# Attention's out projections as three products of high and low parts, and a new order for the end of attention

## The chip, the cores and the metric

The kernel runs on one core of one Trainium2 chip. The metric is the time of one execution on the device, in microseconds. The engines are PE (TensorE), ACT (ScalarE), DVE (VectorE), POOL (GpSimd) and SP (SyncE, which only issues DMAs here). Each runs its own instructions in program order, and they meet at semaphores.

## The reference

```python
x = x + 0.5 * ffn(layernorm(x))     # 2048 tokens of 512; top 2 of 8 experts, 256 wide, all in float32
x = x + attn(layernorm(x))          # 16 query heads, 4 key and value heads of 32, rope, causal
x = x + 0.5 * ffn(layernorm(x))
# attn: q, k, v = x @ wq, x @ wk, x @ wv; rope on q, k
#       softmax(q k^T / sqrt(32), causal) v, heads side by side, then @ wo (512 x 512)
# ffn:  logits = x @ router_w.T; softmax over the top 2; silu(x w1) * (x w2) @ w3 of each
```

The out projection, `out @ wo`, is what the change is about. Its result, added to x, decides which experts each token gets in the second ffn, so it is wanted in nearly full float32.

## The kernel before

The program is five stages: the first router, 39 expert tiles, the projections of Q, K and V, attention with the second router, and 39 expert tiles again. A product of full precision is written in one of two ways. The plain one is a float32 matmul. The other splits both factors into a high part in fp32r (ScalarE's copy that rounds) and a low part (the factor minus the high part) and sums three fp32r matmuls, high x high, high x low and low x high; the experts (L839, L862) are written so.

Attention works through 16 groups G (query block b = G // 4 of 512 tokens, key head G % 4 with its 4 query heads). A group has 4b + 4 tiles, one for each 128 keys. A tile is four steps `score` (PE L1635, then ACT's exp L1754 into P4, of which there are 2 up to group 7 and 4 from group 8), and one `weigh` a tile later (PE L1647, P times V). Where the sums of exps are formed differs: PE (L1665), POOL's `link` adds into CH (L1827, k = 1, 2, 4, 5, 7 and from block 3 on 8, 10), DMA's `onto` adds into CD (L1843), and in group 15 DVE's `pair` (L1891). POOL also masks the four diagonal tiles of each group (L1813). While groups run, PE also computes `top` products for the row maxima of later groups (L997; DVE L1010, L1012); the last one is at 962 us.

At a group's end `out` copies the weighted values to OT and the sums to SM (ACT L1762, L1765), `tsum` turns the sums (PE L1673, DVE reciprocal L1904), `even` spreads them (PE L1682) and DVE multiplies OT (L1914; in group 15 in four pieces, L1918). After a block's fourth group follows its finish: four `proj` of 128 tokens (PE L1702, 4 chunks of the 512 inputs), DVE's add of x (L1877, L1879), statistics, normalization, four `turn` (PE L388, ACT L399), `logits` and `best`.

The order is one hand-written list, `attend_plan`, that each engine's loop walks through, doing its own share of each step. `finish_plan` gives a block's finish, of which one entry is taken per tile, at its second score; the finish of block 0 begins 34 steps after its last group, those of blocks 1 and 2 nine steps after, in the fourth tile of groups 8 and 12. The end of attention (block 3) is written out at the end of `attend_plan`: after the last `weigh` come `out` 15, four splits of weights for the second experts (`split1`: ACT L567 high, then POOL L573 low), `tsum`, `even` and, for each c of 4, `proj`, `norm1` (DVE: statistics, variance; ACT's root L340; DVE's Newton steps and the shift L1952) and `scale1` (ACT L1774); `keep` copies the sum from PSUM to XO (ACT L1781) and frees its bank. `pe_turn` 15 is preceded by 11 filler matmuls (L378).

PSUM's eight banks: `Ring` hands out banks to steps in the order of the plan, from a list that `set_banks` changes; whoever is given a bank waits until its former user has freed it (`pe_take`). Bank 3 holds the weighted values, 4 the sums; scores use three banks, and five from the last `top` on.

OT is two buffers, one for even and one for odd blocks. WO, the weights, is loaded by SP before the first score.

## Time and profile before

| | us |
|---|---|
| three runs | 1288.40, 1294.34, 1295.16 |
| median | 1294.34 |
| profiled execution, its own time | 1291.39 |
| its span, first to last instruction | 1290.1 |
| PE busy in the span | 1198.4 (93%) |
| DVE busy | 891.7 (69%) |
| ACT busy | 665.4 (52%) |
| POOL busy | 599.7 (46%) |
| mean granted TensorE clock | 0.987 of 2.4 GHz |
| attention: first score to the router's logits | 417.5 to 1048.9 |
| PE's out projections, 64 matmuls as 128 records | 57.4 busy, 0.59 each |

The profile has each instruction with its start and duration, and for idle time the work whose end released it. A float32 matmul stands as two records; matmuls overlap, so a step's cost is the distance between starts, not the sum of the durations. Busy shares over the whole span say little about a change in one stage, so the rows below are read by stage.

### The profile page before, as it was taken

What the parts mean: (1) busy time and instruction counts of PE and PEld (TensorE: products, weight loads), DVE (VectorE), ACT (ScalarE), POOL (GpSimd) and SP (SyncE); (2) the same over time, 40 slices, a digit from 0 to 9 for tenths busy, and PEclk for the clock granted to TensorE, in tenths of its full rate; (3) what the DMA queues carried; (4) which work ended last, traced back from release to release, by engine and by line L of the source; (5) the groups of instructions that cost most, each with busy time, mean ns of one, the idle gap of its engine ahead of it and who ended that gap; (6) DMA issues with size and microseconds to landing.
All of it is one profiled execution on the core that took longest, in us unless ns stands there. A gap on an engine that the chain in (4) does not pass through costs nothing.

```text
span 1290.1 us, 22099 instructions
## 1 busy us (share of the span) xinstructions
PE 1198.4 (93%) x7406; PEld 778.3 (60%) x7413; DVE 891.7 (69%) x2100; ACT 665.4 (52%) x1321; POOL 599.7 (46%) x496
## 2 busy tenths in 40 slices
PE   4899999999998999999999999989999978999996
PEld 3578888758776555444545455545444446777774
DVE  7767777679996666476577677677763666666664
ACT  2545555436555554354456565456567853444442
POOL 4845444323210111001436457454764273888886
PEclk9899999999999999999999999999999999999998
DMA  9933333565630032023445844655843263666665
GB/s 331 364 97 107 106 108 108 169 178 107 101 57 5 32 68 35 1 69 67 98 99 147 173 108 99 197 120 146 162 98 67 69 236 85 102 106 101 101 103 78
DMA packets 68557, 148.52 MB, mean 115 GB/s; under 512 B 8832, under 2 KB 29312, under 8 KB 64448
## 3 DMA queue, kind: packets, MB, share of 16 engines
q0 software_dynamic: 35184, 93.34, 34.3%
q1 hardware_dynamic: 33264, 53.77, 12.2%
q8 instruction: 64, 1.05, 0.3%
q14 instruction: 45, 0.37, 0.1%
HBM read 81.28 MB, written 33.55 MB: 89 GB/s over the span
## 4 chain that ended last, share of the span: by engine, by line
PE 61%; DVE 15%; DMA 10%; issue 6%; POOL 4%; ACT 4%; SPq 0%; DVEq 0%; POOLq 0%; ACTq 0%
PE bank L839 10%; PE bank L1635 10%; PE bank L1647 9%; PE bank L997 8%; PE bank L862 6%; PE bank L1702 4%; PE bank L1665 4%; DMA XG<-xn,TK 4%; POOL out L789 3%; DMA out<-Y,DI 3%; DVE PM L1010 3%; DVE bank L1012 2%; PE bank L821 2%; PE bank L1398 2%; DMA CD<-P 1%
## 5 line engine op out<-in xcount | busy, mean ns | idle before, releaser
L1754 ACT ACTIVATE P<-bank 128x512 f32<-128x512 f32 (+3 forms) x640 | 303.6, 535 | 259.3 <-PE bank L1635 252.7
L1010 DVE TENSOR_REDUCE PM<-bank 128x1 f32<-128x512 f32 x384 | 252.8, 686 | 82.6 <-PE bank L997 81.9
L1635 PE MATMUL bank<-Qs,Ks 98*128 98x512 f32 (+3 forms) x640 | 241.0, 407 | 5.1 <-ACT P L1754 2.8
L997 PE MATMUL bank<-Ks,Qs 96*128 96x512 f32 (+3 forms) x640 | 234.4, 387 | 10.8 <-DVE PM L1012 5.3
L1635 PEld LDWEIGHTS bank<-Qs,Ks 98*128 98x128 f32 x640 | 116.8, 190 | 130.8 <-issue 59.5
L1813 POOL TENSOR_SCALAR_AFFINE_SELECT P<-P 128x512 f32<-128x512 f32 x64 | 42.7, 677 | 284.6 <-ACT P L1754 235.2
L1012 DVE CUSTOM_DVE_ANT_0 bank<-bank,KB 128x128 f32<-128x128 f32 (+3 forms) x256 | 124.7, 499 | 56.4 <-PE bank L997 55.8
L997 PEld LDWEIGHTS bank<-Ks,Qs 96*128 96x128 f32 x640 | 121.5, 191 | 57.5 <-DVE PM L1010 17.5
L1647 PE MATMUL bank<-P,V 128*32 128x512 f32 (+3 forms) x1280 | 150.9, 543 | 3.7 <-POOL P L1813 3.7
L1827 POOL TENSOR_TENSOR CH<-CH,P 128x512 f32<-128x512 f32 x108 | 139.2, 1435 | 14.1 <-ACT P L1754 13.3
L789 POOL DMA_INDIRECT out<-Y,DI x78 | 126.1, 1617 | 38.4 <-issue 29.4
L951 DVE TENSOR_TENSOR DL<-W,DH 128x512 fp32r<-128x512 f32 x152 | 98.4, 689 | 40.9 <-issue 20.5
L766 POOL DMA_INDIRECT XG<-xn,TK x78 | 93.5, 1198 | 32.7 <-issue 18.9
L912 ACT CAST DH<-W 128x512 fp32r x152 | 86.7, 618 | 20.3 <-issue 20.3
L839 PE MATMUL bank<-WH,XH 128*128 x312 | 92.3, 417 | 0.9 <-issue 0.6
L839 PE MATMUL bank<-WL,XH 128*128 x312 | 85.7, 396 | 1.4 <-DVE XL L933 1.4
L778 POOL DMA_INDIRECT y<-Y,DI x39 | 40.5, 1039 | 97.3 <-DVE Y L961 97.3
L839 PE MATMUL bank<-WH,XL 128*128 x312 | 85.4, 395 | 0.0
L933 DVE TENSOR_TENSOR XL<-bank,XH 128x512 fp32r<-128x512 f32 x78 | 53.9, 691 | 32.3 <-ACT XH L892 32.1
L898 ACT ACTIVATE G<-bank 128x256 f32<-128x256 f32 x78 | 29.9, 384 | 85.5 <-PE bank L839 85.5
L892 ACT CAST XH<-bank 128x512 fp32r<-128x512 f32 x78 | 45.8, 587 | 43.9 <-PE bank L821 41.2
L839 PEld LDWEIGHTS bank<-WL,XH 128*128 128x128 f32 x312 | 58.6, 188 | 15.9 <-issue 1.8
(195 smaller groups left out, 1978.1 us busy)
## 6 DMA issues: line engine op xcount, KB each, us to landing
CD<-P POOLq DMA_DIRECT2D x17, 1024.0 KB, 7.3
xn<-XN SPq DMA_DIRECT2D x8, 1024.0 KB, 6.5
WR<-L_ffn_w POOLq DMA_DIRECT2D x16, 512.0 KB, 15.6
XO<-y POOLq DMA_DIRECT2D x8, 1024.0 KB, 9.6
WR<-L_ffn_w SPq DMA_DIRECT2D x16, 512.0 KB, 8.4
CD<-P SPq DMA_DIRECT2D x7, 1024.0 KB, 5.2
CD<-CH POOLq DMA_DIRECT2D x7, 1024.0 KB, 6.9
XA<-y POOLq DMA_DIRECT2D x24, 256.0 KB, 4.2
```

Of the source, the lines that this page charges most:

```text
L766: pool.indirect_dma_start(out=x.XG[:, j % NG, :], out_offset=None, in_=g.xnd[f][:, :], in_offset=bass.IndirectOffsetOnAxis(ap=r.TK[:, j:j ...
L789: pool.indirect_dma_start(out=g.out.rearrange("t (h d) -> (t h) d", h=2), out_offset=bass.IndirectOffsetOnAxis(ap=r.DI2[:, h, j:j + 1], ax ...
L839: ins = pe.matmul(bk(g, 2 + j % 2), part[:, k * P:k * P + P], w[:, bass.ds(ev[j] * 2048 + k * 512, 512)], start=(n == 0 and k == 0), stop= ...
L912: act.copy(x.DH[:, k, :], W.W3[:, bass.ds(e * 1024 + k * 512, 512)]).then_inc(s("dh"), 1)
L951: ins = dve.tensor_tensor(x.DL[:, k, :], W.W3[:, bass.ds(e * 1024 + k * 512, 512)], DHf[:, k, :], ALU.subtract)
L997: pe.matmul(bk(g, bank)[:, 0:n], g.Qs[b][0:96, G % 4 * 4 + h, c * P:c * P + P], g.Ks[0:96, G % 4, k * BQ:k * BQ + n], start=True, stop=Tru ...
L1010: dve.tensor_reduce(dst, bk(g, bank)[:, 0:n], AX.X, ALU.max).then_inc(s(f"free{bank}"), 1)
L1012: dve.tensor_tensor_reduce(out=bk(g, bank)[:, 0:n], in0=bk(g, bank)[:, 0:n], in1=g.KB[:, CB_MASK + BQ - n:CB_MASK + BQ], scale=1.0, scalar ...
L1635: pe.matmul(bk(g, bank)[:, o:BQ], g.Ks[0:98, G % 4, k * P:k * P + P], g.Qs[G // 4][0:98, G % 4 * 4 + j, o:BQ], start=True, stop=True).then ...
L1647: ins = pe.matmul(bk(g, 3)[32 * h:32 * h + 32, o:BQ], g.V[:, k, q * HD:q * HD + HD], a.P4[buffer_of(n)][:, h, o:BQ], start=(k == 0), stop= ...
L1754: act.activation(a.P4[buffer_of(n)][:, j, o:BQ], bk(g, score_bank(g, i))[:, o:BQ], ACT.Exp, scale=scale).then_inc(s("exp"), 1)
L1827: ins = pool.tensor_tensor(to[:, h, :], two[:, h, :], one[:, h, :], ALU.add)
```

## The change

The out projections of blocks 1 to 3 are computed by three fp32r products each. During block 0's finish ACT copies the four chunks of WO to WOH and POOL subtracts to WOL; WOH lies over OT0, WOL over WO. From then on all blocks use OT1, with its low part OL in the same place and its high part OH in place of the turned xT1. The step `part` makes a quarter of OH (ACT) and of OL (POOL). Blocks 1 and 2 have a quarter per 128 tokens, and their projections begin two tiles later than the parts; block 3 has a quarter per group, after the tiles (14, 4), (14, 9) and (15, 6), and group 15's own quarter is made by DVE, in `late`, from the bank where `even` wrote.

At the end, the first three chunks of block 3's projections are steps of their own (`lead`): those of c = 0 in the three tiles before the last one's `weigh`, the others around `tsum`, `even` and the later projections. `proj` 3 is left with the chunk of group 15. `norm1` is cut in two, with `var1` (statistics, variance, root) ahead; `late`, `var1`, `norm1`, `split1`, `keep` and `turn` stand in a new order, and the ring's lists of banks are others. SP's loads of WO and XO count on one semaphore, `rows`. POOL's `part` in the diff is cut; it picks the same quarter as ACT's. The walks over the plan call the new functions, and ACT's root stands at `var1`.

```diff
@@ memory(nc, ctx, g)
     a.XO = low("XO", [P, 4, D])
-    a.OTs = [ot0, low("OT1", [P, 4, BQ])]
+    a.WOH = nc.alloc_sbuf_tensor_at("WOH", [P, 4, D], F32R, offset=A_T + 16 * KB1)
+    a.WOL = nc.alloc_sbuf_tensor_at("WOL", [P, 4, D], F32R, offset=A_T + 24 * KB1)
+    a.OL = nc.alloc_sbuf_tensor_at("OL", [P, 4, BQ], F32R, offset=low.at)
+    ot1 = low("OT1", [P, 4, BQ])
+    a.OTs = [ot0, ot1, ot1, ot1]
+    a.OH = nc.alloc_sbuf_tensor_at("OH", [P, 4, 4, P], F32R, offset=low.at + 8 * KB1)
@@ finish_plan(b)
-    todo = [[("proj", b, c)] for c in range(4)]
-    todo += [[("stats", b, c)] for c in range(4)]
+    if b:
+        todo = [[("part", b, 0)], [("part", b, 1)], [("part", b, 2), ("proj", b, 0)], [("part", b, 3), ("proj", b, 1)],
+                [("proj", b, 2)], [("proj", b, 3)]]
+        todo += [[("stats", b, c)] for c in range(4)]
+    else:
+        todo = [[("proj", b, c)] for c in range(4)]
+        todo += [[("stats", b, c), ("wo", c)] for c in range(4)]
@@ attend_plan(g)
+        if (G, k) in ((14, 4), (14, 9), (15, 6)):
+            plan.append(("part", 3, {4: 0, 9: 1, 6: 2}[k]))
+        if len(TILES) - 4 <= n < len(TILES) - 1:
+            put(4 * n + 7, ("lead", 0, n + 4 - len(TILES)))
-    plan += [("weigh", len(TILES) - 1), ("out", 15), ("up1", 4), ("split1", 0), ("split1", 1), ("split1", 2), ("split1", 3), ("tsum", 15), ("even", 15)]
-    for c in range(4):
-        plan += [("proj", 3, c), ("norm1", c), ("scale1", c)] + ([("turn", 12 + c - 2), ("keep", c - 2)] if c >= 2 else [])
-    plan += [("turn", 14), ("turn", 15), ("keep", 2), ("keep", 3), ("split1", 4), ("split1", 5), ("split1", 6), ("split1", 7)]
+    plan += [("weigh", len(TILES) - 1), ("out", 15), ("up1", 4), ("split1", 0), ("split1", 1), ("split1", 2)]
+    plan += [("lead", 1, 0), ("tsum", 15), ("lead", 1, 1), ("even", 15), ("late", 0), ("late", 1), ("lead", 1, 2)]
+    plan += [("proj", 3, 0), ("var1", 0), ("late", 2), ("proj", 3, 1), ("norm1", 0), ("scale1", 0), ("late", 3), ("var1", 1), ("split1", 3)]
+    plan += [("lead", 2, k) for k in range(3)] + [("proj", 3, 2), ("norm1", 1), ("scale1", 1), ("var1", 2), ("turn", 12), ("keep", 0)]
+    plan += [("lead", 3, k) for k in range(3)] + [("proj", 3, 3), ("norm1", 2), ("scale1", 2), ("var1", 3), ("turn", 13)]
+    plan += [("norm1", 3), ("scale1", 3), ("keep", 1), ("turn", 14), ("turn", 15), ("keep", 2), ("keep", 3)]
+    plan += [("split1", 4), ("split1", 5), ("split1", 6), ("split1", 7)]
-        if step == ("proj", 3, 0):
-            ring.set_banks([5, 6, 7, 0, 2, 1], 5)
+        if step == ("turn", 12):
+            ring.set_banks([6, 0, 7, 5], 3)
         elif step == ("out", 15):
-            ring.set_banks([5, 6, 7])
+            ring.set_banks([5, 6, 0, 1, 2], 4)
+        elif step[0] == "lead" and step[2] == 0:
+            ring.take(("proj", 3, step[1]))
@@ pe_attend(g)
+    def times_wo(bank, c, k):
+
+        pe.matmul(bk(g, bank), a.OH[:, c, k, :], a.WOH[:, k, :], start=(k == 0), stop=False)
+        pe.matmul(bk(g, bank), a.OH[:, c, k, :], a.WOL[:, k, :], start=False, stop=False)
+        return pe.matmul(bk(g, bank), a.OL[:, k, c * P:c * P + P], a.WOH[:, k, :], start=False, stop=(k == 3))
+
+    def lead(c, k):
+
+        bank, _ = g.ring.where[("proj", 3, c)]
+        if k == 0:
+            pe_take(g, ("proj", 3, c))
+            if c == 0:
+                b0, u0 = g.ring.where[("even", 14)]
+                pe.wait_ge(s(f"free{b0}"), u0 + 1)
+            else:
+                pe.wait_ge(s("exp"), 4 * len(TILES))
+            pe.wait_ge(s("ol"), 15)
+        times_wo(bank, c, k)
+
+    def last_proj(key):
+
+        _, b, c = key
+        bank, _ = g.ring.where[key]
+        if c < 3:
+            pe.wait_ge(s("ol"), c + 16)
+        else:
+            b0, u0 = g.ring.where[("even", 15)]
+            pe.wait_ge(s(f"free{b0}"), u0 + 1)
+        times_wo(bank, c, 3).then_inc(s(f"full{bank}"), 1)
+
     def proj(key):
...
+        if b:
+            pe.wait_ge(s("ol"), 4 * b + c + 1)
+            for k in range(4):
+                ins = times_wo(bank, c, k)
+            ins.then_inc(s(f"full{bank}"), 1)
+            return
         for k in range(4):
-            ins = pe.matmul(bk(g, bank), a.OTs[b % 2][:, k, c * P:c * P + P], a.WO[:, k, :], start=(k == 0), stop=(k == 3))
+            ins = pe.matmul(bk(g, bank), a.OTs[b][:, k, c * P:c * P + P], a.WO[:, k, :], start=(k == 0), stop=(k == 3))
         ins.then_inc(s(f"full{bank}"), 1)
@@ act_attend(g)
         if b >= 2 and G % 4 == 0:
-            bank, use = g.ring.where[("proj", b - 2, 3)]
+            bank, use = g.ring.where[("proj", b - 1, 3)]
             act.wait_ge(s(f"full{bank}"), use + 1)
-        act.copy(a.OTs[b % 2][:, G % 4, :], bk(g, 3)).then_inc(s("oT"), 1)
+        act.copy(a.OTs[b][:, G % 4, :], bk(g, 3)).then_inc(s("oT"), 1)
+    def part(b, i):
+
+
+        b0, u0 = g.ring.where[("even", 4 * b + 3 if b < 3 else 12 + i)]
+        act.wait_ge(s(f"free{b0}"), u0 + 1)
+        if i == 0:
+            b1, u1 = g.ring.where[("best", 1, b - 1)]
+            act.wait_ge(s(f"full{b1}"), u1 + 1)
+        if b < 3:
+            act.copy(a.OH[:, i, :, :], a.OTs[b][:, :, i * P:i * P + P]).then_inc(s("oh"), 1)
+        else:
+            act.copy(a.OH[:, :, i, :], a.OTs[b][:, i, :].rearrange("p (c n) -> p c n", c=4)).then_inc(s("oh"), 1)
+
+    def weights(k):
+        if k == 0:
+            bank, use = g.ring.where[("proj", 0, 3)]
+            act.wait_ge(s(f"full{bank}"), use + 1)
+        act.copy(a.WOH[:, k, :], a.WO[:, k, :]).then_inc(s("oh"), 1)
@@ pool_attend(g)
+    def part(b, i):
+
+        pool.wait_ge(s("oh"), 4 * b + i + 1)
...
+        pool.tensor_tensor(to, one, high.bitcast(F32), ALU.subtract).then_inc(s("ol"), 1)
+
+    def weights(k):
+        pool.wait_ge(s("oh"), k + 1)
+        pool.tensor_tensor(a.WOL[:, k, :], a.WO[:, k, :], a.WOH[:, k, :].bitcast(F32), ALU.subtract).then_inc(s("ol"), 1)
@@ dve_attend(g)
-        for c in range(4):
-            v = slice(c * P, c * P + P)
-            ins = dve.tensor_tensor(o[:, v], o[:, v], bk(g, bank)[:, v], ALU.mult)
-            ins.then_inc(s("norm") if c < 3 else s(f"free{bank}"), 1)
+
+    def late(c):
+
+        bank, use = g.ring.where[("even", 15)]
+        o, v = bk(g, bank)[:, c * P:c * P + P], slice(c * P, c * P + P)
+        dve.tensor_tensor(o, a.OTs[3][:, 3, v], o, ALU.mult).then_inc(g.dv.sem, 1)
+        dve.wait_ge(g.dv.sem, g.dv.up())
+        dve.tensor_copy(a.OH[:, c, 3, :], o).then_inc(g.dv.sem, 1)
+        dve.wait_ge(g.dv.sem, g.dv.up())
+        ins = dve.tensor_tensor(a.OL[:, 3, v], o, a.OH[:, c, 3, :].bitcast(F32), ALU.subtract)
+        ins.then_inc(s("ol") if c < 3 else s(f"free{bank}"), 1)
```

## Rows read from the trace of the kernel before

**Rows 1.** Busy time of each engine in two stretches: busy us (instructions), clock, DMA share, GB/s.
```profile
820.00:860.00 40.00, 38.25 (x170) 19.64 (x169) 27.67 (x63) 17.87 (x34) 27.48 (x23) 1.00 0.48 114
965.00:1015.00 50.00, 47.19 (x334) 19.76 (x334) 25.35 (x42) 41.01 (x86) 16.00 (x16) 1.00 0.26 53
```
**Rows 2.** POOL's timeline, groups 12 and 14: start, us, what; idle before and its releaser.
```profile
842.83 0.85 POOL L1843 DMA_DIRECT2D CD<-P  x1 [5.13 <-ACT P L1754]
...
951.08 10.07 POOL L1827 TENSOR_TENSOR CH<-CH,P 128x512 f32<-128x512 f32 x8 [0.53 <-ACT P L1754]
...
961.73 10.26 POOL L1827 TENSOR_TENSOR CH<-CH,P 128x512 f32<-128x512 f32 x8
...
972.52 5.23 POOL L1827 TENSOR_TENSOR CH<-CH,P 128x512 f32<-128x512 f32 x4
977.47 0.85 POOL L1813 TENSOR_SCALAR_AFFINE_SELECT P<-P 128x512 f32<-128x512 f32 x1
```
**Rows 3.** PE's timeline, the diagonal tiles of group 14.
```profile
978.47 1.06 PE L1647 MATMUL bank<-P,V 128*32 128x512 f32 x8 [1.20 <-POOL P L1813]
...
986.22 1.07 PE L1656 MATMUL bank<-CD,ones 128*32 128x512 f32 x8 [0.36 <-DMA CD<-CH]
```
**Rows 4.** PE's timeline from the last tiles to the router's logits.
```profile
1016.63 1.06 PE L1647 MATMUL bank<-P,V 128*32 128x512 f32 x8 [0.64 <-POOL P L1813]
...
1022.57 0.43 PE L1647 MATMUL bank<-P,V 128*32 128x128 f32 x8 [0.33 <-POOL P L1813]
...
1025.91 1.08 PE L1682 MATMUL bank<-K,R 128*32 128x128 f32 x32 [0.42 <-DVE R L1904]
1027.49 10.54 PE L1702 MATMUL bank<-WO,OT 128*128 128x512 f32 x24 [0.50 <-DVE OT L1918]
...
1043.93 2.32 PE L378 MATMUL bank<-KB 128*128 128x512 bf16 x10
1047.12 0.63 PE L388 MATMUL bank<-K,XN 128*128 128x128 f32 x4 [0.87 <-ACT XO L1781]
1048.91 1.54 PE L413 MATMUL bank<-xT,RT 128*32 128x128 f32 x32 [1.16 <-ACT XO L1781]
```
**Rows 5.** PE's timeline, four fp32r products of an expert.
```profile
1078.24 1.10 PE L839 MATMUL bank<-WL,XH 128*128 x4
```
**Rows 6.** ACT's timeline, the last scaling and what follows.
```profile
1045.24 0.78 ACT L1774 ACTIVATE XN<-bank,sm 128x512 f32<-128x512 f32 x1 [1.23 <-DVE sm L1952]
...
1046.38 0.60 ACT L1781 COPY XO<-bank 128x512 f32<-128x512 f32 x1
...
1048.27 1.08 ACT L1781 COPY XO<-bank 128x512 f32<-128x512 f32 x2
```
**Rows 7.** DVE's timeline behind the last `even`.
```profile
1027.06 0.88 DVE L1918 TENSOR_TENSOR OT<-OT,bank 128x128 f32<-128x128 f32 x4 [1.20 <-PE bank L1682]
1031.20 0.70 DVE L1879 TENSOR_TENSOR bank<-bank,XO 128x512 f32<-128x512 f32 x1 [3.26 <-PE bank L1702]
...
1034.63 0.70 DVE L1879 TENSOR_TENSOR bank<-bank,XO 128x512 f32<-128x512 f32 x1
...
1036.74 0.16 DVE L327 RECIPROCAL sm<-sm 128x1 f32<-128x1 f32 x1 [0.27 <-ACT sm L340]
```
**Rows 8.** PE's timeline, a hole in the stage of the projections of Q, K, V.
```profile
412.48 3.96 PE L1415 MATMUL bank<-K,NA 128*96 128x128 f32 x20 [2.67 <-DVE NA L1271]
```
**Rows 9.** Stretches as in the first group; the 1.00 or 0.50 is the clock.
```profile
413.00:414.00 1.00, 1.00 (x7) 0.93 (x5) 0.00 (x0) 0.78 (x3) 0.00 (x0) 0.50 0.00 0
416.00:417.00 1.00, 0.44 (x5) 0.18 (x2) 0.00 (x0) 0.96 (x2) 0.00 (x0) 1.00 0.00 0
672.00:673.00 1.00, 1.00 (x3) 0.77 (x3) 0.41 (x3) 0.82 (x2) 0.47 (x1) 0.50 0.00 0
677.00:678.00 1.00, 1.00 (x13) 0.59 (x6) 0.00 (x0) 0.25 (x1) 0.00 (x0) 0.50 0.00 0
1046.00:1048.00 2.00, 0.88 (x6) 0.42 (x4) 0.00 (x0) 1.68 (x5) 0.00 (x0) 1.00 0.55 214
```

More of the change, by code:

```diff
@@ L1594, in attend_plan @@
             ring.set_banks(ids, len(ids) - 1)
-        if step[0] in ("top", "proj", "tsum", "even", "found"):
+        if step[0] in ("top", "tsum", "even", "found") or step[0] == "proj" and step[1] < 3:
             ring.take(step)
+        elif step[0] == "lead" and step[2] == 0:
+            ring.take(("proj", 3, step[1]))
         elif step[0] in ("turn", "logits", "best"):
@@ L1689, in proj @@
         if b == 0 and c == 0:
-            pe.wait_ge(s("wo"), 16)
+            pe.wait_ge(s("rows"), 32)
         b0, u0 = g.ring.where[("even", 4 * b + 3)]
@@ L1720, in pe_attend @@
             even(step)
+        elif kind == "proj" and step[1] == 3:
+            last_proj(step)
         elif kind == "proj":
             proj(step)
+        elif kind == "lead":
+            lead(step[1], step[2])
         elif kind == "turn":
@@ L1792, in act_attend @@
             out(step[1])
+        elif kind == "part":
+            part(step[1], step[2])
+        elif kind == "wo":
+            weights(step[1])
         elif kind == "foundcopy":
@@ L1843, in onto @@
         pool.dma_start(a.CD[:], one[:], accum_op=ALU.add).then_inc(s("onto"), 16)
-    for step in g.plan:
-        if step[0] == "score" and step[2] == 3:
+    def part(b, i):
+        pool.wait_ge(s("oh"), 4 * b + i + 1)
+        if b < 3:
+            to, one = (t[:, :, i * P:i * P + P] for t in (a.OL, a.OTs[b]))
+            high = a.OH[:, i, :, :]
+        else:
+            to, one = (t[:, i, :].rearrange("p (c n) -> p c n", c=4) for t in (a.OL, a.OTs[b]))
+            high = a.OH[:, :, i, :]
+        pool.tensor_tensor(to, one, high.bitcast(F32), ALU.subtract).then_inc(s("ol"), 1)
+    def weights(k):
+        pool.wait_ge(s("oh"), k + 1)
+        pool.tensor_tensor(a.WOL[:, k, :], a.WO[:, k, :], a.WOH[:, k, :].bitcast(F32), ALU.subtract).then_inc(s("ol"), 1)
+    for step in g.plan:
+        if step[0] == "part":
+            part(step[1], step[2])
+        elif step[0] == "wo":
+            weights(step[1])
+        elif step[0] == "score" and step[2] == 3:
             n = step[1]
@@ L1858, in pool_attend @@
             else:
-                pool.wait_ge(s("xo"), 16 * b + 16)
+                pool.wait_ge(s("rows"), 16 * b + 32)
             pool.dma_start(a.XO[:], g.yd[T * h + BQ * b:T * h + BQ * b + BQ, :].rearrange("(i p) d -> p i d", p=P),
@@ L1944, in dve_attend @@
             dve_scale(g, g.R1, step[1], a.XO, step[2])
-        elif kind == "norm1":
-            c, sm = step[1], g.R1.sm
+        elif kind == "late":
+            late(step[1])
+        elif kind == "var1":
+            c = step[1]
             dve.wait_ge(s("last"), c + 1)
@@ L1950, in dve_attend @@
             dve_variance(g, g.R1, c, c + 1, 3 + c)
+        elif kind == "norm1":
+            c, sm = step[1], g.R1.sm
             dve_solve(g, g.R1, c, c + 1, 3 + c)
@@ L1962, in sp_attend @@
     all_projected(g, sp.wait_ge)
-    sp.dma_start(a.WO[:], d["L0_attn_wo"].rearrange("(k p) n -> p k n", p=P)).then_inc(s("wo"), 16)
+    sp.dma_start(a.WO[:], d["L0_attn_wo"].rearrange("(k p) n -> p k n", p=P)).then_inc(s("rows"), 16)
     def rows(t, b):
@@ L1985, in sp_attend @@
                 sp.wait_ge(s("stored"), 16 * b)
-            sp.dma_start(a.XO[:], rows(d["L0_attn_x"].rearrange("b t d -> (b t) d"), b)).then_inc(s("xo"), 16)
+            sp.dma_start(a.XO[:], rows(d["L0_attn_x"].rearrange("b t d -> (b t) d"), b)).then_inc(s("rows"), 16)
         elif kind == "store":
```

12 lines of the change are left out of this document (3 added, 9 removed).

## The prediction, made before the changed kernel was run

> **What bounds the kernel now.** I read the busy time by stage first, then PE's timeline at the out projections, then POOL's, and last every engine from the final score tile to the router's logits. While tops still run, PE is busy 38.25 of 40 us and no other engine comes near; from 965 to 1015 us, once they are gone, ACT has 41 of 50 us and PE 47 [rows 1]. So whatever PE saves before 965 us shortens the span, one for one, unless a later wait takes it back. Two places are not PE's. In group 14 POOL works from 951 to 978 us without a break and PE and ACT wait for it [rows 2, 3]. From the last score on, the work is a chain through ACT, PE and DVE, and its steps decide.
>
> **Projections of blocks 1 and 2 (a gain).** The plain form of one projection leaves eight records of PE; 24 records, three projections, take 10.54 us, each 0.59 long, so they start (10.54 - 0.59) / 23 = 0.433 us apart and a projection is 3.46 us of PE [rows 4]. The new form is twelve fp32r products of 128 x 512. The experts already run that form: four take 1.10 us, the last 0.395 of it, so one costs (1.10 - 0.395) / 3 = 0.235 us [rows 5], and twelve 2.82. Saved: 0.64 us each, 5.1 us for the eight of blocks 1 and 2. Bounds: 0 (if DVE's tops or ACT take over at once) and 5.6 us. I take 5.1, as PE is the busy engine there.
>
> **What that form adds.** ACT gets 15 copies of 128 x 512 (4 weights, 8 for blocks 1 and 2, 3 for block 3), POOL 15 subtractions. A copy is 0.6 us by ACT's COPY to XO [rows 6]; a POOL add of that size is 5.23 / 4 = 1.3 us [rows 2]. In block 0's finish POOL only masks, and ACT has more than half of the time free; in groups 8 and 12 the parts come at tiles 3 to 6, where POOL still waits (5.13 us idle just before 842.83 [rows 2]), so four parts, 5.2 us, fill holes. Behind them on POOL stand links 4, 5 and 7, whose buffers are wanted four tiles later, and the first projection moves two tiles back to wait for its parts. Cost 0, up to 1.5 us without that cover. The shared OT1 makes group 8's and 12's copy wait for projection 3 of the block before; that is over three tiles earlier. The joined semaphore of SP's loads, and the finish that is two tiles longer, cost nothing: stores and XO loads have tens of us.
>
> **Parts of block 3 in group 14 (a loss).** Two of the three parts are planned after tiles 4 and 9 of group 14. There POOL has 10.07, 10.26 and 5.23 us of adds with two DMA issues between them, end to end, and then the mask that PE waits 1.20 us for [rows 2, 3]. Queued behind the parts are links 5, 7, 8 and 10, the DMA adds, the masks. Two parts at 1.25 us are 2.5 us; the later wait for the merged sum (0.36 us on PE) is there before and is absorbed [rows 3], so +2.1. Bounds 0 and 3.0. The third part is in group 15, where POOL only masks.
>
> **First products in the last tiles (a loss ahead, a gain behind).** `lead` 0 is 9 of projection 0's 12 products, three in each of the last tiles: 3 x 0.70 = 2.1 us. Two holes of PE take 0.64 and 0.33 of it [rows 4]; +1.1. Projection 1's three leads lie in the waits around `tsum` and `even`; the middle one is 0.70 long against a hole of 0.4 and so delays `even` by 0.2. Together +1.3, bounds +0.6 and +2.1.
>
> **From `even` 15 to the last shift (a gain).** Before, DVE begins at 1027.06, the first sum waits for the whole projection 0 (3.26 us idle) and starts at 1031.20, and the last shift is out at 1045.24, 18.2 us after 1027.06 [rows 6, 7]. One chunk is 3.43 us of DVE (1031.20 to 1034.63), 0.27 us of the next one is the wait for the root [rows 7]. Behind, DVE is the bound: four `late` of three operations at 0.28 and two self waits, 0.93 each, 3.7; four chunks 13.7; three root waits, now under other work, -0.8: 16.6 us. PE, three products after each `late`, stays ahead of it. So -1.6.
>
> **From the last shift to the logits (a loss).** Here the banks matter. Going through the ring by hand: projection 1 sits in bank 5, projection 3 in bank 0, and turns 12 to 15 get 6, 7, 5, 6, the logits 0. So turn 14 needs `keep` 1, which ACT does only after `scale_last` 3; the 11 filler matmuls of turn 15 are behind turn 14 on PE; and the logits need `keep` 3, not 2. Before, turn 14 and the filler (2.32 us for ten) ran under the last chunk, turn 15 began 1.88 us after the shift and the logits 3.67 us after it [rows 4, 6]. Behind: scale 0.7, keep 0.6 and hand-over, turn 14 at +1.4; turn 0.63 and filler 2.4, turn 15 at +4.45; from there 1.8 as before and one more copy of 0.5: logits at +6.8. That is +3.1; bounds +1.5 and +3.6.
>
> **TensorE's clock.** On that schedule PE has nothing between turn 13 (about 12.5 us after `even`) and turn 14 (18.0), 5.5 us. After a hole of 2.67 us before 412.48 the granted clock was 0.50, that is 1.2 GHz, at 413 us, and 1.00 again at 416 [rows 8, 9]. Turn 14 and filler, 3.0 us, would so run at half for up to 3.3 us: +1.3 (0 to 1.7). The Trainium skill (TensorE: Matmul & The Clock Gate, Part 1: The HAM clock gate) says that the half-rate state is the default and activity lifts it, in two levels only; by that rule this change, which leaves PE less to do at the end, pays for it in the work that follows. The trace agrees: 0.50 in the rows named, and nothing between the levels but slices that hold both.
>
> **Sum.** -5.1 + 2.1 + 1.3 - 1.6 + 3.1 + 1.3 = +1.1 us. The profiled execution took 1291.39 us; it lies 2.95 us under the median of the three runs, 1294.34, and these spread over 6.8 us. The profile's differences carry over to the median: 1295.4 us.
>
> **Rivals.**
> (A) POOL and the end cost nothing. If POOL's parts in group 14 pass under ACT's own waits, and the turns come in a better order than I read, the body's gain stays: -5.1 + 0 + 1.3 - 1.6 + 1.5 = -3.9, 1290.4 us. With the body at 5.6, the leads at 0.6 and nothing at the turns it would be -6.6, 1287.7 us, the only way to be clearly faster. For it: PE is the bound nearly everywhere. Against: POOL's unbroken row in group 14.
> (B) Slower: the clock falls in both holes of the end. PE also has 2 us without work before turn 12, which waits for the first `scale_last`, and `lead` 3 stands behind turn 12. In its place the loss is this: a half clock that lasts 6 us, as at 672 and 677 us [rows 9], doubles `lead` 3 with its last products (2.8 us more, 1.9 of it past DVE's own time), and at the other hole turn 14, the filler, turn 15 and the logits (2.4 + 0.5 + 0.5 + 1.5 = 4.9). 6.8 in place of 1.3: +6.6, 1300.9 us. It decides once the clock falls before `lead` 3. Before, the end kept 1.00 through holes of 0.9 us [rows 4, 9], which speaks against it; the 2 us hole speaks for it.
> (C) The change does not bring its gain in the body: DVE, 27.67 of 40 us busy [rows 1], or ACT behind the new copies holds PE, and 5.1 becomes 0: +6.2, 1300.5 us. Little speaks for it, as PE hardly waits there now.
>
> **How the numbers follow.** Forecast 0.50, (A) 0.28, (B) 0.14, (C) 0.08. About 0.5%, 6.5 us, is what a measurement of this kernel can tell from no change: 1287.9 to 1300.8. All of the forecast's case, most of (A) and half of (B) and (C) lie within. Range 1287.5 to 1302: down to (A) at its best, up to (B), a little over. Faster 0.14, same 0.70, slower 0.16.
>
> **What would show it.** Right: PE's out projections in groups 8 and 12 as twelve records at 0.235 us; POOL's row in group 14 ends 2.5 us later and PE's wait for the mask grows from 1.20 to some 3.7; the first sum of block 3 starts 2 us after `even` 15 where it was 4.1; the last shift is 16.6 us after it; PE idle over 5 us before turn 14, waiting for ACT's copy to XO, then a granted clock of 0.5. Wrong: a PE wait for POOL's low part at a projection in group 8 or 12; PE at DVE's mercy in the body; turn 14 directly after turn 13.

## The result, and the profile after

The changed kernel takes 1298.23 us (median of ten runs, 1296.07 to 1300.47), the kernel before 1292.70 us in the same session (ten runs, 1288.40 to 1296.12). The ratio is 1.004, with an interval of 1.0026 to 1.0053. The forecast was 1295.4, between 1287.5 and 1302; the time lies in the range and within 0.5%. Its direction, a little slower, is right. The change itself was forecast at 1.1 us and measured at 5.5. That the time still lies within 0.3% of the forecast is partly luck: the forecast started from the median of three runs, 1294.34, and ten runs of the kernel before have 1292.70. The last experiment says how little a ratio of this size can carry.

The page of the changed kernel, its busy times and one row of its slices:

```profile
span 1297.5 us, 22237 instructions
PE 1198.1 (92%) x7454; PEld 794.7 (61%) x7461; DVE 895.9 (69%) x2108; ACT 672.0 (52%) x1336; POOL 621.7 (48%) x511
...
PEclk8899999999998999999999999999998979999999
```

Before, the span was 1290.1 us and PE busy for 1198.4. So PE works as long as before although the projections got shorter: it does some of its work at half the clock. ACT has 15 operations more, POOL 15.

The first two rows below answer to [rows 1]: the same stretch of group 12 and of groups 14 and 15, counted from the sums (`tsum`) before them. The columns are those of [rows 1]. In the first PE is as busy as before, and POOL has 3.7 us more (31.15 for 27.48), where the low parts are. In the second PE has lost 2.6 us of work in 50 (44.60 for 47.19), and its clock is 0.93. The last two lie in the end of attention.

```profile
819.00:859.00 40.00, 38.30 (x194) 24.10 (x193) 28.31 (x62) 20.28 (x39) 31.15 (x26) 1.00 0.51 124
960.50:1010.50 50.00, 44.60 (x309) 18.27 (x305) 21.27 (x34) 37.32 (x80) 20.13 (x19) 0.93 0.28 58
...
1044.00:1046.00 2.00, 1.54 (x6) 1.17 (x8) 0.00 (x0) 0.68 (x2) 1.28 (x1) 0.50 0.76 295
1046.00:1048.00 2.00, 2.00 (x6) 0.71 (x5) 0.00 (x0) 0.00 (x0) 0.00 (x0) 0.50 0.60 229
```

One profile of each isn't enough for differences of a few us, so both kernels were profiled again, before three times and the changed one once. Landmarks on PE's timeline cut the span into stages; a stage `gN` runs from the transposed sum (`tsum`) of group N - 1 to that of group N. The experts' first is PE's first turn of gated values in the second expert stage. Worked out from those timelines, in us, as means of four profiles and of two:

```
stage                        before   after   difference   forecast
start to first score          417.3   417.5      +0.2          0
first score to tsum 0          17.0    17.8      +0.7          0
g1 to g6 (same work)          150.9   150.9       0            0
g7                             34.9    34.5      -0.4          0
g8                             58.1    54.7      -3.4        -2.6
g9                             47.1    49.6      +2.5          0
g10, g11 (same work)           82.5    82.4       0            0
g12                            72.8    67.8      -5.0        -2.6
g13                            57.9    59.3      +1.3          0
g14                            47.7    51.6      +3.9        +2.1
g15                            36.4    37.5      +1.1        +1.1
tsum 15 to logits              24.1    26.6      +2.6        +3.0
logits to experts' first       32.4    31.9      -0.6          0
second experts and end        210.7   213.3      +2.7          0
span                         1289.9  1295.4      +5.6        +1.1
```

So the body (g8, g9, g12, g13) gave 4.6 us, forecast 5.1; group 14 took 3.9 in place of 2.1; group 15 and the end took 3.6 in place of 4.1. What the forecast had no term for at all is the last stage, +2.7.

PE's timeline of the changed kernel, a projection in group 8 (columns as in [rows 3]). These are twelve records where there were eight, the first three and the last shown:

```profile
635.91 0.40 PE L1709 MATMUL bank<-WOH,OH 128*128 128x512 f32 x1
636.15 0.40 PE L1710 MATMUL bank<-WOL,OH 128*128 128x512 f32 x1
636.38 0.39 PE L1711 MATMUL bank<-WOH,OL 128*128 128x512 f32 x1
...
638.43 0.39 PE L1711 MATMUL bank<-WOH,OL 128*128 128x512 f32 x1
```

From 635.91 to the next score at 638.65 it is 2.74 us; the forecast had 2.82.

PE's timeline in the groups 9 and 14 of the changed kernel. The first two rows are the transposed sum that ends group 8 and the transposed row maxima in group 9; before waited 0.42 and 0.82 us there. The third answers to the first of [rows 3], 1.20 there; the 0.36 that followed it is gone. The last row is a stretch of PE alone behind it (its busy time, the clock, DMA share, GB/s).

```profile
677.31 0.89 PE L1694 MATMUL bank<-K,SM 128*128 128x128 f32 x4 [2.64 <-DVE PM L1017]
...
697.22 0.60 PE L1066 MATMUL bank<-K,M 128*8 128x128 f32 x4 [2.70 <-DVE M L1057]
...
976.40 1.93 PE L1668 MATMUL bank<-P,V 128*32 128x512 f32 x8 [4.53 <-POOL P L1892]
...
976.00:981.00 5.00, 4.60 (x20) 0.50 0.77 159
```

In front of the first two waits stands DVE's normalization of block 1: at the end of group 8 DVE waits for ACT's root, and in group 9 a scaling takes 1.68 us, where most take 0.54, ahead of the last reductions.

```profile
675.55 0.18 DVE L319 RECIPROCAL sm<-sm 128x4 f32<-128x4 f32 x1 [1.10 <-ACT sm L347]
...
693.13 1.68 DVE L361 TENSOR_SCALAR XN<-XO,mv,sm 128x512 f32<-128x512 f32 x1
```

The eight products at 976.40 take 1.93 us where eight of the same form took 1.06 in [rows 3]: half the clock. POOL's timeline of the same place, with the two low parts (L1933) in a row that was already full [rows 2]:

```profile
951.62 1.29 POOL L1933 TENSOR_TENSOR OL<-OT,OH 128x512 fp32r<-128x512 f32 x1
952.86 5.00 POOL L1906 TENSOR_TENSOR CH<-CH,P 128x512 f32<-128x512 f32 x4
...
958.39 10.35 POOL L1906 TENSOR_TENSOR CH<-CH,P 128x512 f32<-128x512 f32 x8
...
969.23 1.56 POOL L1933 TENSOR_TENSOR OL<-OT,OH 128x512 fp32r<-128x512 f32 x1
970.47 5.20 POOL L1906 TENSOR_TENSOR CH<-CH,P 128x512 f32<-128x512 f32 x4
975.37 0.89 POOL L1892 TENSOR_SCALAR_AFFINE_SELECT P<-P 128x512 f32<-128x512 f32 x1
```

The end of attention, which answers to [rows 4]. PE of the changed kernel from turn 12 to the logits:

```profile
1035.03 0.66 PE L395 MATMUL bank<-K,XN 128*128 128x128 f32 x4 [1.51 <-ACT XN L1849]
...
1040.05 0.63 PE L395 MATMUL bank<-K,XN 128*128 128x128 f32 x4 [1.62 <-ACT XO L1856]
1044.24 1.09 PE L395 MATMUL bank<-K,XN 128*128 128x128 f32 x4 [3.56 <-ACT XO L1856]
1045.55 4.35 PE L385 MATMUL bank<-KB 128*128 128x512 bf16 x10 [0.22 <-issue]
...
1051.98 1.54 PE L420 MATMUL bank<-xT,RT 128*32 128x128 f32 x32 [1.65 <-ACT XO L1856]
```

Turn 14 (1044.24) waits for `keep` 1, which ACT does behind the last scaling. Then ten filler matmuls take 4.35 us; in [rows 4] they took 2.32. DVE and ACT (which answer to [rows 6, 7]), the same kernel: the first product with the normalizer (`late` 0), the first sum, the sums of chunks 2 and 3, the last shift, the last scaling, and `keep` 1.

```profile
1027.82 0.30 DVE L2018 TENSOR_TENSOR bank<-OT,bank 128x128 f32<-128x128 f32 x1 [1.41 <-PE bank L1703]
...
1029.81 0.70 DVE L1977 TENSOR_TENSOR bank<-bank,XO 128x512 f32<-128x512 f32 x1 [0.20 <-PE bank L1711]
...
1035.94 0.69 DVE L1977 TENSOR_TENSOR bank<-bank,XO 128x512 f32<-128x512 f32 x1
1036.54 0.15 DVE L334 RECIPROCAL sm<-sm 128x1 f32<-128x1 f32 x1
...
1038.62 0.69 DVE L1977 TENSOR_TENSOR bank<-bank,XO 128x512 f32<-128x512 f32 x1
...
1042.59 0.21 DVE L2060 TENSOR_SCALAR sm<-mv,sm 128x1 f32<-128x1 f32 x1
...
1042.84 0.78 ACT L1849 ACTIVATE XN<-bank,sm 128x512 f32<-128x512 f32 x1 [0.76 <-DVE sm L2060]
1043.52 0.58 ACT L1856 COPY XO<-bank 128x512 f32<-128x512 f32 x1
```

The first sum starts 1.99 us after `late` 0, and the last shift is out at 1042.80, 15.0 us after it. A chunk is 1038.62 - 1035.94 = 2.68 us of DVE, for 3.43 before. Of that 3.43, DVE waited 0.43 for the root, in this row of the kernel before:

```profile
1033.46 0.16 DVE L327 RECIPROCAL sm<-sm 128x1 f32<-128x1 f32 x1 [0.43 <-ACT sm L340]
```

### The profile page after: what moved, and what is told of

Its sections match the earlier page's. It is cut to its first block, busy times and chain, and to the rows that moved or that the text cites. A ratio compares the mean times of both kernels' runs of the same rounds, so it can differ in the third digit from the quotient of the medians.

```text
span 1297.5 us, 22237 instructions
## 1 busy us (share of the span) xinstructions
PE 1198.1 (92%) x7454; PEld 794.7 (61%) x7461; DVE 895.9 (69%) x2108; ACT 672.0 (52%) x1336; POOL 621.7 (48%) x511
## 3 DMA queue, kind: packets, MB, share of 16 engines
q8 instruction: 64, 1.05, 0.3%
## 4 chain that ended last, share of the span: by engine, by line
PE 63%; DVE 16%; DMA 7%; issue 6%; POOL 5%; ACT 3%; SPq 0%; POOLq 0%; DVEq 0%; ACTq 0%
PE bank L846 10%; PE bank L1656 10%; PE bank L1668 9%; PE bank L1004 8%; PE bank L869 6%; PE bank L1686 4%; DMA out<-Y,DI 4%; DMA XG<-xn,TK 3%; DVE bank L1019 2%; DVE PM L1017 2%; POOL out L796 2%; PE bank L828 2%; POOL CH L1906 2%; PE bank L1405 2%; PE bank L1703 1%
## 5 line engine op out<-in xcount | busy, mean ns | idle before, releaser
L796 POOL DMA_INDIRECT out<-Y,DI x78 | 128.3, 1644 | 40.8 <-issue 30.5
L911 ACT CAST GH<-bank 128x256 fp32r<-128x256 f32 x76 | 28.3, 373 | 78.1 <-PE bank L856 71.9
```

Of the source, the lines that this page charges most:

```text
L796: pool.indirect_dma_start(out=g.out.rearrange("t (h d) -> (t h) d", h=2), out_offset=bass.IndirectOffsetOnAxis(ap=r.DI2[:, h, j:j + 1], ax ...
```

## The experiments

**Both kernels again, unchanged.** These give the stages above their spread.

> The kernel before, once more, for a second profile of it: the changed kernel's profile is 5.2 us longer in the second expert stage and 2.0 us in group 0, where the two run the same code. Theory (the stages vary from execution to execution by clock and gathers): the second expert stage, from the first to the last turn of gated values, is not 196.3 us again but 197 to 200, and group 0 ends 17 to 19 us after the first score. Rival (something in the changed kernel makes them longer): 196.3 +- 0.5 and 16.8 +- 0.3 us again.

> The kernel before, a third profile. The second expert stage, the same code in all kernels, took 196.3 and 197.2 us in two profiles of the kernel before and 197.6 to 201.5 in eight of the changed kernel and its variants. Theory (its gathers land at varying times, and the eight are chance): one of the three profiles of this call's kernels before falls above 198.5 or the changed kernel's below 198. Rival (the changed kernel really makes it longer): 196 to 197.5 here, 199 to 201 in the changed kernel.

> The kernel before, a fourth profile: as for the third, the second expert stage above 198.5 us by the one theory, 196 to 197.5 by the other. Groups 8 and 9 together 105 to 107 us, group 14 47.6 us and from group 15's sums to the logits 24.1 us again by both.

> The changed kernel, a second profile: group 14 51.5 us with a hole of 4.5 us before its first masked tile, and a half clock there and before the logits again (26.6 us from group 15's sums to the logits); the second expert stage below 198 us if its length is chance, 199 to 201 if the changed kernel makes it longer.

Measured: 1289.06, 1291.14 and 1292.86 us for before, 1294.64 us for the changed kernel; spans 1287.8, 1289.9, 1291.6 and 1293.4. Most stages agree to 0.1 us between profiles of one kernel; of those that don't, first score to `tsum` 0, g7, g8 and g12 differ by where the granted clock happened to be at half; the second experts differ by up to 3 us among the profiles of before. The changed kernel's first profile has 18.8 us between the first score and `tsum` 0, its second 16.8, with the same instructions. Group 14 repeats: 51.5 and 51.7, with 4.53 and 4.54 us of wait for the mask. So do g9 (49.6, 49.5), g13 (59.3, 59.3) and the end (26.6, 26.7). Those are of the change; the first +0.7 is not. Of the theories on the second experts' stage, neither holds cleanly: a fourth profile of before has 198.8 us from the first to the last turn of gated values, above the 198.5 that speaks for chance, and the changed kernel's second has 200.7, which speaks for the change.

**The low parts of block 3 out of group 14, into group 15.**

```
-        if (G, k) in ((14, 4), (14, 9), (15, 6)):
+        if (G, k) in ((15, 1), (15, 4), (15, 7)):
```

> The changed kernel with the three parts of block 3 all planned in group 15 (after tiles 1, 4 and 7), where GpSimd has nothing else to do but mask. Theory (GpSimd's two extra subtractions in group 14 push the mask that TensorE waits for, and the longer hole also lowers the granted clock): the wait before the weigh of group 14's first masked tile falls from 4.5 us to about 1.2, the half clock at 974 to 981 us is gone, and the kernel is about 3.9 us faster than the changed kernel, 1294.3 us, still 1 to 2 us above the kernel before. Rival (the loss in group 14 comes from TensorE being ahead by the projections' gain and would appear wherever the parts are): the time stays at 1298 us and the same wait is there. Second rival (in group 15 the subtractions meet VectorE's pair sums and ScalarE, 41 of 50 us busy): the mask of group 15 comes later by 1 to 2 us and takes back half of the gain.

Measured: 1295.01 us (12 runs), before 1292.17; ratio 1.0021 (1.0006 to 1.0036). Group 14 went from 51.6 to 49.9 us and the wait for the mask to 2.43, but group 15 from 37.5 to 40.1, some of it under a half clock (995 to 999 us). With the same edit in the third kernel below it is 48.5 and 38.8. This profile is of the slowest of the twelve executions (1302.15 us). So part of what POOL gave back in group 14, in this profile all of it, went in group 15, as the second rival said, and its rows show where. The median is near the theory's 1294.3, but its wait of 1.2 us is not there (2.43), and the half clock in group 14 is shorter, not gone (978 to 982 us). DVE in group 15 adds pairs of tiles, both inputs from SBUF; these are its rows here (duration in ns, least, median and most), and the same operation before:

```profile
L1989 DVE TENSOR_TENSOR CD<-CD,P x40: 635/684/1770, 994.9 to 1024.7; 128x512 f32<-128x512 f32 x40
L1989 DVE TENSOR_TENSOR CD<-P,P x4: 683/688/1756, 991.3 to 993.1; 128x512 f32<-128x512 f32 x4
```
```profile
L1891 DVE TENSOR_TENSOR CD<-CD,P x40: 643/686/1120, 991.7 to 1017.6; 128x512 f32<-128x512 f32 x40
```

An add of 0.69 us takes up to 1.77 when POOL subtracts beside it, and POOL's subtraction goes from 1.29 to as much as 1.79 (at 1010.36). One such add (between 991.29 and 994.78) delays the reciprocal of group 14's sums, and PE then waits for it:

```profile
995.17 1.48 PE L1703 MATMUL bank<-K,R 128*32 128x128 f32 x32 [1.80 <-DVE R L2002]
```

That wait was 0.87 us in the changed kernel. The Trainium skill (SBUF — State Buffer, section 🔬 SBUF: two separate sides) says that DVE and GpSimd share a port pair by an exclusive lock, held for a whole instruction, and that a DVE operation with two SBUF inputs meets it against a GpSimd operation that reads SBUF. With that the trace agrees: 1.77 us is 0.69 and most of one subtraction of 1.29.

**`keep` 1 ahead of the last scaling.**

```
-    plan += [("norm1", 3), ("scale1", 3), ("keep", 1), ("turn", 14), ...
+    plan += [("keep", 1), ("norm1", 3), ("scale1", 3), ("turn", 14), ...
```

> The changed kernel with one step moved: ScalarE's copy keep 1 stands right after turn 13, ahead of the last scaling. Theory (turn 14 waits for bank 5, which keep 1 frees after the last scaling; TensorE stands idle before it, and its clock falls under turn 14, the fillers and turn 15): turn 14 starts 1.5 us earlier, turn 15 and the logits 1.5 us earlier with the clock unchanged, up to 4 us earlier if the clock stays at 1.00; 1294 to 1297 us. Rival (the chain is set by VectorE's statistics and what comes behind them, the bank doesn't matter): logits at the same distance, 9.1 us, from the last shift, 1298 us.

Measured: 1294.79 us (12 runs), ratio 1.0020 (1.0000 to 1.0040). From `tsum` 15 to the logits it is 24.1 us, as before the change, in place of 26.6. PE's timeline, turns 14 and 15 and the logits:

```profile
1041.11 0.63 PE L395 MATMUL bank<-K,XN 128*128 128x128 f32 x4 [2.05 <-ACT XO L1856]
1041.57 4.22 PE L385 MATMUL bank<-KB 128*128 128x512 bf16 x11
1045.63 0.60 PE L395 MATMUL bank<-K,XN 128*128 128x128 f32 x4
1047.89 1.54 PE L420 MATMUL bank<-xT,RT 128*32 128x128 f32 x32 [1.65 <-ACT XO L1856]
```

Turn 14 starts at 1041.11, just as the last shift is done (1041.19), where that of the changed kernel starts 1.44 us behind it. Yet the eleven fillers still take 4.22 us. PE alone over two stretches (its busy time, the clock, DMA share, GB/s):

```profile
1040.00:1042.00 2.00, 0.89 (x6) 0.92 0.03 8
1042.00:1044.00 2.00, 2.00 (x6) 0.50 0.55 212
```

The clock is at half, and turn 15 waits behind them.

**Both together.**

> The changed kernel with both: the three parts of block 3 in group 15 and keep 1 right after turn 13. Theory: the two losses are apart from each other and their removal adds up, 5 to 7 us under the changed kernel, 1291 to 1293 us, level with the kernel before or 1 us under it. Rival (the loss lies elsewhere, in the second expert stage, which was 5.2 us longer in the changed kernel's profile): 1297 us or more.

Measured: 1296.62 us (12 runs), ratio 1.0032 (1.0015 to 1.0048). Group 14 is 48.5 us and group 15 38.8, the end 25.1; together 112.4, where the changed kernel has 115.7, the first alone 116.0 and the second 113.5. The profile says 3.3 us won against the changed kernel; the medians say 1.6, and put it behind both single edits. The expected 5 to 7 us did not come. The three intervals overlap, so the medians alone don't say that the two edits fail to add up; it is a hint that something of 1 to 3 us moves them that isn't in these stages.

**Plain projections for blocks 1 and 2 again**, with the copies and subtractions kept; the low parts are left out of those eight products, so their value is rounded more.

```
-            for k in range(4):
-                ins = times_wo(bank, c, k)
+            for k in range(4):
+                ins = pe.matmul(bk(g, bank), a.OH[:, c, k, :].bitcast(F32), a.WOH[:, k, :].bitcast(F32), ...)
```

> The changed kernel, with the projections of blocks 1 and 2 as plain float32 products of the high parts (four matmuls in place of twelve fp32r ones; the low parts are still made but left out of these products). Theory (TensorE sets the pace in groups 8 and 12, so 0.64 us for each of eight projections is a real gain of the change): 5.1 us slower than the changed kernel, 1303.3 us. Rival (VectorE or ScalarE sets the pace there, the gain is eaten at once): the same time as the changed kernel, 1298 us.

Measured: 1298.06 us (6 runs), ratio 1.0045 (1.0029 to 1.006). Group 8 is 57.5 us for 54.7 and group 12 70.6 for 67.8: 2.75 and 2.8 us for four projections each, 0.69 per projection, 5.5 in all. Group 14 gives 2.3 back: it is 49.2 us, and PE's waits in it are

```profile
968.53 1.48 PE L1656 MATMUL bank<-Qs,Ks 98*128 98x512 f32 x3 [0.95 <-ACT P L1811]
...
977.83 1.07 PE L1668 MATMUL bank<-P,V 128*32 128x512 f32 x8 [1.35 <-POOL P L1893]
```

1.35 us for the mask in place of 4.53, and no half clock at 977 (there is one at 970, behind the 0.95, for half as long as the changed kernel has it). The mask itself is not earlier: PE's product behind it starts 39.95 us after `tsum` 13 here and 39.97 in the changed kernel, and POOL's row ahead of it is the same to 0.1 us. What differs is that ACT stood 1.73 us for a DMA that read P, so PE waited and ran at half clock ahead of the mask, where POOL's row hides it, and ran at full clock behind. So the 2.3 us are the price of the half clock behind the mask, and they are not a part of the projections' gain. By the stages the theory holds; by the median, which is that of the changed kernel and not 1303.3, the rival does, and the 3.2 us left of the 5.5 aren't in the medians (see the last experiment).

**The low parts early in group 14**, one of them in a place where POOL has not filled up yet.

```
-        if (G, k) in ((14, 4), (14, 9), (15, 6)):
+        if (G, k) in ((14, 0), (14, 3), (15, 6)):
```

> The changed kernel with the parts of block 3 planned after tiles 0 and 3 of group 14 and tile 6 of group 15: the first falls in GpSimd's hole before the first link of group 14, the second behind it, still ahead of the unbroken row. Theory (GpSimd's row in group 14 is what costs; in group 15, as the runs before showed, the subtractions meet VectorE's pair sums and cost 0.6 to 1 us each): the stretch from the sums of group 13 to those of group 14, 51.5 us in the changed kernel and 47.6 before, is 48 to 49 us, and that of group 15 stays at 37.5; about 2.5 to 3 us faster than the changed kernel, 1295.5 us. Rival (any subtraction ahead of link 10 costs its full length): 50.5 us or more.

Measured: 1294.51 us (12 runs), before 1293.33; ratio 1.0016 (1.0000 to 1.0032). The wait for the mask is 3.15 us for 4.53, group 14 50.7 for 51.6, group 15 37.3. Group 14 is what the rival said (50.5 or more) and not the theory's 48 to 49, but not for its reason: the product behind the mask starts 38.4 us after `tsum` 13, 0.8 later than before and not 2.3. The rest is the half clock at 971 and a wait of 1.57 us for the merged sum.

**With it, `keep` 1 ahead and the fillers at turn 14, not 15.**

```
-            if step[1] == 15:
+            if step[1] == 14:
```

> As the run before (parts of block 3 after (14, 0), (14, 3), (15, 6)), and at the end keep 1 right after turn 13 and the eleven filler matmuls ahead of turn 14 rather than turn 15, so that they fill TensorE's hole. Theory (the hole before turn 14 lowers the clock and the fillers behind it then take 4.3 us on the path): no half clock between 1038 and 1049 us, turn 15 within 2 us of the last shift, from the sums of group 15 to the logits 21 to 22 us where the kernel before has 24.1 and the changed one 26.6; 1291 to 1292 us, 1 us under the kernel before. Rival (the clock falls anyway, in the hole before turn 12): 24 us or more.

Measured: 1291.27 us (12 runs, of which one took 2869.49 us, and nothing on record says why; the ratio is without it), ratio 0.9974 (0.9956 to 0.9992). From `tsum` 15 to the logits it is 20.6 us, 6.3 less than without these two lines and 3.5 less than the kernel before.

**With all of that, finishes of blocks 1 and 2 one tile shorter.**

```
-        todo = [[("part", b, 0)], [("part", b, 1)], [("part", b, 2), ("proj", b, 0)], ...
+        todo = [[("part", b, 0), ("part", b, 1)], [("part", b, 2), ("proj", b, 0)], ...
```

> As the run before, and the finish of blocks 1 and 2 one tile shorter: parts 0 and 1 in one tile, then part 2 with projection 0, part 3 with projection 1. Theory (in group 9 the changed kernel's finish, two tiles later, puts VectorE's normalization next to its solving of the row maxima, and TensorE waits 2.7 us for them and loses its clock): group 9, 49.5 us in the changed kernel and 47.1 before, moves by at least 1 us either way, and groups 8 and 9 together, 104.4 against 106.7, change; 1290 us if it moves off. Rival (the wait is set by the order of tops alone): 49.5 +- 0.5 us again.

Measured: 1286.79 us (12 runs), before 1293.33; ratio 0.9960 (0.9945 to 0.9974). This version beats both kernels; it is 6.5 us under the kernel before, twice the difference that the last experiment finds with nothing moved. Group 9 is 48.1 us for 49.6, group 12 69.4 for 67.8, group 14 49.1; the wait at the end of group 8 is gone, and the clock is 1.00 over 698 to 701, where the changed kernel has 0.51, and through group 14. PE's waits in groups 9 and 14, then its end of attention:

```profile
692.52 0.60 PE L1066 MATMUL bank<-K,M 128*8 128x128 f32 x4 [0.83 <-DVE M L1057]
...
971.22 1.06 PE L1668 MATMUL bank<-P,V 128*32 128x512 f32 x8 [1.95 <-POOL P L1892]
...
1033.90 0.63 PE L395 MATMUL bank<-K,XN 128*128 128x128 f32 x4 [1.59 <-ACT XO L1856]
1034.37 2.54 PE L385 MATMUL bank<-KB 128*128 128x512 bf16 x11
1036.74 0.60 PE L395 MATMUL bank<-K,XN 128*128 128x128 f32 x4
1037.53 0.66 PE L395 MATMUL bank<-K,XN 128*128 128x128 f32 x4 [0.19 <-ACT XN L1849]
1039.84 1.54 PE L420 MATMUL bank<-xT,RT 128*32 128x128 f32 x32 [1.65 <-ACT XO L1856]
```

The same eleven fillers take 2.54 us: they now stand right behind turn 13, where PE would have had its hole, and the clock holds. Turn 15 follows the last scaling at once.

**A kernel in which nothing moves.** All kernels of the changed family lose time in the second stage of experts, whose code is that of before. One row goes with it: POOL's issues of the scatter-add, 1622 to 1633 ns on the mean in four profiles of before, 1644 to 1662 in nine others. The edit asks whether it is the length of POOL's instruction stream.

```
         elif step[0] == "split1" and step[1] < NE - 1:
             pool_low(g, 1, step[1])
+    for _ in range(30):
+        pool.wait_ge(s("exp"), 1)
```

> The kernel before with nothing changed but GpSimd's instruction stream, which gets 30 more instructions at the end of attention: waits on a count that was reached long ago, so that nothing in the schedule moves. It asks where the second stage of experts loses time in every kernel of the changed family (199.5 us on the mean of nine profiles against 197.2 of four before), with the same code and the same work in it. One row goes with it: GpSimd's scatter-add takes 1622 to 1633 ns on the mean in the four profiles of before and 1644 to 1662 in the nine others. Theory L (the length or place of GpSimd's instructions, which the 15 subtractions and their waits moved): the scatter-add's mean is 1645 ns or more here, the stage is near 199.5 us, and the median is some 2 us over before. Theory D (something else of the change, or chance): the mean stays at 1620 to 1635 ns, the stage within 196.3 to 198.7 us, and the median within 1 us of before.

Measured: POOL's scatter-adds, first of this kernel and then of the changed one profiled again (count and mean in ns stand behind the bar):

```profile
L789 POOL DMA_INDIRECT out<-Y,DI x71 | 115.2, 1622 | 33.3 <-issue 27.3 <-DVE Y L961 5.2 <-DMA out<-Y,DI 0.8
```
```profile
L796 POOL DMA_INDIRECT out<-Y,DI x69 | 114.5, 1659 | 32.8 <-issue 28.9 <-DVE Y L968 3.0 <-DMA out<-Y,DI 0.9
```

1622 ns, and 196.8 us from the first to the last turn of gated values: the row and the stage are those of before, so theory L falls. No stage of this profile lies more than some 0.1 us outside the four of before (logits to experts' first 32.9 us for 32.2 to 32.8). But the median is 1294.51 us (12 runs), before 1291.33 (17 runs); ratio 1.0024, with an interval of 1.0008 to 1.004. That is 3.2 us over, where theory D had it within 1 us. Thirty waits that were met long ago, at most 0.5 us in the profile, go with 3 us in the medians by an interval that excludes 1. Whether that comes of building the kernel anew or of chance in the drawing of runs isn't shown. Either way, no ratio here of 1.001 to 1.003 may be read as an effect of its edit, nor 0.997.

## Why the prediction was right, and where its steps were not

**Projections of blocks 1 and 2.** Right. 0.69 us each by the plain variant, forecast 0.64; twelve records at 0.23 as expected, no wait for a low part. Rival (C), no gain in the body, falls.

**What that form adds in the body: cost 0.** Wrong at the end of group 8 and in group 9; elsewhere in the body no new wait for POOL or ACT stands out. "The finish that is two tiles longer" was held to cost nothing because of stores and XO loads; the step left out that the block's normalization on DVE moves too. It now lies beside the reductions that PE waits for at the end of group 8 and in group 9: waits of 2.64 and 2.70 us where 0.42 and 0.82 stood, with the clock at half behind each (678 to 681 and 698 to 701). One tile less brought group 9 from 49.6 to 48.1 and the second wait to 0.83, and the first is gone. Group 13's +1.3 is mostly not a loss but work that moved: PE does four of block 2's turns in it, where before two of them ran in group 12. With one tile less it does three, and is 0.6 us longer. The wait for the row maxima in it is 1.04 for 0.74. The body's sum of 4.6, forecast 5.1, is right by luck in part: the products gave 5.5, and 4.1 us of new waits for DVE were nearly balanced by what the forecast had no term for. In group 8 these are a wait of 1.34 us for ACT that is gone and a half clock about 671 us in three of the four profiles of before (1.5 us on the mean; the profile without it took 56.6): -2.75 - 1.3 - 1.5 + 2.2 = -3.4. In group 12 they are the two turns that went to group 13, 0.8 us of waits that went away with the new places, and a half clock in one of the four profiles.

**Parts in group 14, +2.1.** The mechanism is right, the size is not. The mask came 2.3 us later behind `tsum` 13 (PE's product behind it at 39.97 us for 37.63), forecast 2.5. PE's wait grew by 3.3, but 0.9 of that only takes the place of a wait for ACT (`mT`) that stood ahead of it before. What was missing is the clock: it fell in the hole of 4.5 us, and the tiles behind it ran at half, 976 to 981 us. From that product to the end of the group it is 11.6 us for 10.0, although 0.6 us of small waits are gone. I had counted the clock for the end of attention only. With the wait at 1.35 in the plain variant, and at 1.95 in the best one, it doesn't fall there.

**Leads in the last tiles, +1.1 and +0.2.** Right: group 15 is 0.9 to 1.1 us longer in all seven profiles with one part in it, and `even` starts 1.26 us after `tsum` for 1.05.

**From `even` 15 to the last shift, -1.6.** Better than forecast: 15.0 us from `late` 0, forecast 16.6. The term that was mis-sized is the chunk: 2.68 us in place of 3.43 less 0.27. 0.16 of that is a misreading: the 3.43 held 0.43 of waiting for the root (the row at 1033.46), the 0.27 was the next chunk's, so a chunk without waits was 3.00. The other 0.32 is the order. With `var1` and `norm1` apart, DVE has operations of two chunks in turn; the reciprocal starts 0.60 us after the start of a sum of 0.69 us, where before the statistics that read such a sum started 0.73 after it. I had credited the change with the root's wait alone.

**From the last shift to the logits, +3.1, and the clock, +1.3.** The order of banks, the wait of turn 14 for `keep` 1 and the fillers behind it are as read by hand. Turn 14 starts 1.44 us after the shift, forecast 1.4. Logits come 9.2 us after it (1051.98 - 1042.80), forecast 6.8 and 1.3. PE's hole before turn 14 was 3.56 us, where I had over 5: turn 13 ran later than I had it, behind a hole of 1.6. Still the clock fell, and the fillers at half clock cost 2.03 us more than in [rows 4], and turn 14 0.46 more, where the clock term had 1.3 for all. The two errors (1.6 too slow, 1.1 too fast) nearly cancel.

**Rivals.** (A), POOL and the end cost nothing, falls with 4.53 us at the mask. (B) asked for the clock to fall before `lead` 3; it didn't: the leads at 1035.44 run 0.23 apart. What fell instead was group 14's.

**The second experts, +2.7.** No term. Four profiles of before have 208.9 to 212.1 us from the first turn of gated values to the end of the span, nine of the family 210.9 to 213.7, means 210.7 and 212.4; so some 1.7 us seem to belong to the family. It isn't the length of POOL's stream. It is there with plain projections too (scatter-add 1655 ns), so not a matter of those products. The three longest of the nine have the clock at half once more, near 1190 us; the other six and those of before don't. That is a part of the difference at most; the cause stays open.

**How sure.** The stages show where time went; the total is less certain than its interval says. The stages count +5.6 us between the kernels, the medians +5.5, but a kernel with nothing moved differs by +3. That the change is slower in the stages of attention (+2.6 us from `tsum` 6 to the logits, its gain included) rests on two profiles, 464.0 and 464.1 us, against 460.7 to 463.8 in four of before; that it is slower by 0.4% on the clock is likely, not shown.

## What to carry to other kernels

Look for the rows in which another engine works without a break before pricing work that is added to it: there it comes out at nearly full length (2.3 us for two parts), and the hole that it makes in the bounding engine can cost as much again in clock (2.3 us). Put filler work where the engine would otherwise idle, not behind the wait that makes it idle; here the same eleven matmuls cost 4.22 us in one place and 2.54 in the other, and two lines turned a loss of 2.6 us into a gain of 3.5. And for effects under 0.3%, profile both kernels several times by stages, and measure a kernel in which nothing moves, before a ratio is believed.

## What the runs showed of the hardware

- A DVE add of two SBUF tiles of 128 x 512 took 1.67 to 1.80 us where it met a POOL subtraction (six of them in e1_parts15 and e3_both) and 0.69 without; a scale-and-shift of 128 x 512 from SBUF (L361) took 1.68 in group 9, beside POOL's run of adds, and 0.54 by the median. Before, I had priced POOL's parts by POOL's time alone.
- PE's clock in group 14 stayed at 1.00 behind a wait for the mask of 1.20, 1.35 or 1.95 us and was at half behind 2.40, 3.15 or 4.53. But it also fell behind 0.95 in the plain variant (970 us) and behind 2.05 in the end of attention, and stayed behind 1.59 there. And behind one and the same wait of 1.34 us in group 8 of the kernel before (671 us) it fell in three profiles and stayed in the fourth. The length of the last wait alone doesn't tell it.
- POOL's issue of one and the same scatter-add is 1578 ns by the median in every kernel, but a part of them takes 1.8 to 2.1 us, 7 to 10 of 78 in the profiles of before and 12 to 16 in those of the changed family; which ones do differs from run to run.
